# When the keys of short attention blocks are loaded: key loads separated from query loads

## The reference

```python
raw = jnp.einsum('bhid,bhjd->bhij', q, k)
scores = sips_alpha[0] * jnp.tanh(raw / sips_beta[0])
scores = scores + lam * hamming[:, None, :, :]      # soft_bits @ soft_bits.T / 2
scores = scores + lat                               # hexc @ Mh @ hexc.T / 6, per head
scores = jnp.where(causal[None, None], scores, -jnp.inf)
attn = jax.nn.softmax(scores, axis=-1)
out = jnp.einsum('bhij,bhjd->bhid', attn, v)
```

## Time and profile before

| | |
|---|---|
| median of three executions | 1880.96 us |
| profiled execution | 1876.1 us |
| its span, first to last instruction | 1874.3 us |
| TensorE busy | 1736.5 us, 93% |
| VectorE busy | 1309.0 us, 70% |
| ScalarE busy | 1232.2 us, 66% |
| GpSimd busy | 620.1 us, 33% |
| mean granted clock of TensorE | 0.955 |
| moved by DMA | 288.49 MB, 154 GB/s on the mean |

### The profile page before, as it was taken

One profiled execution on the slowest core, in us unless ns is written; L12 is line 12 of the kernel. 1 busy time (PEld: TensorE's weight loads), 2 busy tenths in 40 slices (PEclk: granted clock), 3 DMA queues, 4 the chain that ended last, 5 costly groups with the idle time before them and its releaser, 6 DMA issues. The chain is left out here.

```text
span 1874.3 us, 35368 instructions
## 1 busy us (share of the span) xinstructions
PE 1736.5 (93%) x11140; PEld 1041.4 (56%) x11141; DVE 1309.0 (70%) x2675; ACT 1232.2 (66%) x1260; POOL 620.1 (33%) x715
## 2 busy tenths in 40 slices
PE   4798999999999988999999999899559999999997
PEld 1343434434334433333433334388459999999997
DVE  6467888878888866778877877644646666666664
ACT  1177999999999977789999999633513333333332
POOL 0745251432542453243140201237612222222222
PEclk8778999999999989899999999999879999999998
DMA  4689796676863397676575580172256776767773
GB/s 164 184 218 183 163 173 136 138 148 138 185 112 94 88 182 188 135 158 141 118 158 107 116 179 33 56 233 84 92 189 198 198 197 196 198 198 200 198 202 76
DMA packets 183562, 288.49 MB, mean 154 GB/s; under 512 B 20832, under 2 KB 114144, under 8 KB 181280
## 3 DMA queue, kind: packets, MB, share of 16 engines
q1 hardware_dynamic: 168096, 264.92, 56.4%
q0 software_dynamic: 13440, 17.97, 5.6%
q10 hardware_dynamic: 1920, 4.23, 0.6%
HBM read 218.09 MB, written 68.96 MB: 153 GB/s over the span
## 5 line engine op out<-in xcount | busy, mean ns | idle before, releaser
L1298 DVE SCALAR_TENSOR_TENSOR probs<-probs,scal,bil_ps 128x512 f32<-128x512 f32 (+1 forms) x1152 | 789.4, 715 | 239.2 <-PE bil_ps L1140 187.8
L1219 ACT ACTIVATE probs<-probs 128x2048 f32<-128x2048 f32 (+1 forms) x288 | 522.7, 1815 | 82.6 <-DVE probs L1298 82.0
L1212 ACT ACTIVATE probs<-raw_ps 128x2048 f32<-128x2048 f32 (+1 forms) x288 | 509.1, 1768 | 38.4 <-PE raw_ps L1122 28.6
L1140 PE MATMUL bil_ps<-u_mv,w_st 50*128 50x512 f32 (+3 forms) x1280 | 467.6, 454 | 33.9 <-DVE probs L1298 23.4
L1140 PEld LDWEIGHTS bil_ps<-u_mv,w_st 50*128 50x128 f32 x1280 | 200.1, 188 | 515.1 <-DVE probs L1298 428.3
L2020 ACT ACTIVATE rows_sb<-fc_ps,b 128x128 f32<-128x128 f32 x576 | 160.8, 368 | 345.6 <-DVE hid_lo L2052 304.7
L1159 PE MATMUL o_ps<-probs,v_sb 128*32 128x512 f32 (+3 forms) x2560 | 301.0, 552 | 0.1
L1122 PE MATMUL raw_ps<-q_mv,k_st 64*128 64x512 f32 (+3 forms) x1280 | 271.9, 396 | 13.3 <-ACT probs L1212 9.0
L1976 PE MATMUL fc_ps<-modrow,rows_sb 128*128 128x128 f32 x2304 | 271.6, 277 | 0.0
L1976 PEld LDWEIGHTS fc_ps<-modrow,rows_sb 128*128 128x128 f32 x2304 | 265.5, 194 | 0.0
L1949 POOL DMA_INDIRECT out<-modrow,token x72 | 125.4, 1742 | 379.8 <-DVE modrow L2085 374.0
(11 more groups left out here) (233 smaller groups left out, 1564.4 us busy)
## 6 DMA issues: line engine op xcount, KB each, us to landing
rows_sb<-in_w SPq DMA_DIRECT2D x72, 1024.0 KB, 4.9
q_mv<-q_split SPq DMA_DIRECT2D x128, 128.0 KB, 8.6
k_st<-k_split SPq DMA_DIRECT2D x48, 256.0 KB, 8.7
rows<-x_rows SPq DMA_DIRECT2D x72, 130.0 KB, 2.1
v_rows<-rows_sb SPq DMA_DIRECT2D x8, 1024.0 KB, 7.3
o_t<-o_sb SPq DMA_DIRECT2D x32, 256.0 KB, 7.9
k_st<-k_split SPq DMA_DIRECT2D x16, 512.0 KB, 8.7
v_sb<-v_rows SPq DMA_DIRECT2D x8, 1024.0 KB, 14.7
```

What stands on the lines that cost most here:

```text
L1140: mm = pe.matmul(bil_ps[:, hd % 2, column:column + width], codes(kt)[row:row + BIAS_ROWS, :], u_mv[row:row + BIAS_ROWS, p, hd // 2, query: ...
L1212: act.activation(probs[:, s % NBUF, :, first:BLK], raw_ps[:, :, first:BLK], ACT.Tanh).then_inc(tanh_ready, 1)
L1219: act.activation(scores, scores, ACT.Exp).then_inc(exp_ready, 1)
L1298: dve.scalar_tensor_tensor(scores, scores, scal[:, ALPHA:ALPHA + 1], bil_ps[:, hd % 2, first:BLK], ALU.mult, ALU.add).then_inc(sum_ready, 1)
```

## The change

Keys get loads of their own. Three things change with it.

First, where they lie: in a block with c = 0 the iterations of head groups 0 and 1 use columns 0 to 511 of their side, those of groups 2 and 3 use columns 512 to 1023. With c = 1, groups 0 and 1 use the upper half (columns 1024 to 2047), groups 2 and 3 the lower. Longer blocks use the side as before. KEYS_FREE gives for each iteration the last one before it that used any of its columns; the load waits for that one's raw scores, where it waited for iteration it - 2.

Second, when: the keys of iterations 2 to 5 stand at the same steps (0, 2, 5, 8), with no wait for TensorE. Those of 18 and 19 move from steps 143 and 146 to 128 and 143, those of 20 and 21 from 149 and 152 to 137 and 146. For all others step and wait are the same. The queries stay at the steps and behind the waits where keys and queries were.

Third, semaphores: keys_in has six, by iteration number modulo 6, and the queries have two of their own, so TensorE waits for two at an iteration's start. The keys wait for the stores of keys only, the queries for the stores of queries.

```diff
-KEYS_AT = {max(LAST[it - 2] - PE_LEAD, 0): it for it in range(2, len(ITERS))}
+QUERIES_AT = {max(LAST[it - 2] - PE_LEAD, 0): it for it in range(2, len(ITERS))}
+N_SETS = 6
+def keys_column(it):
+    i, g = ITERS[it]
+    return {0: g // 2 * BLK, 1: (1 - g // 2) * 2 * BLK}.get(BLOCKS[i][1], 0)
+def keys_used(it):
+    first = keys_column(it) // BLK
+    return set((it % 2, n) for n in range(first, first + BLOCKS[ITERS[it][0]][1] + 1))
+KEYS_FREE = {it: max([before for before in range(it) if keys_used(before) & keys_used(it)], default=-1)
+             for it in range(len(ITERS))}
+    step = LAST[it - 2] - PE_LEAD
+    if i == NBLK + 1 and g < 2:
+        stored = max(s for s in STORE_AT if (i, "Q3") in STORE_AT[s])
+        step = max(LAST[KEYS_FREE[it]] + 3, stored + 3)
+    elif i == NBLK and g >= 2:
+        step = LAST[KEYS_FREE[it]] - PE_LEAD + 3
+    KEYS_AT.setdefault(max(step, 0), []).append(it)
...
             def load_keys(it):
-                if it >= 2:
-                    sp.wait_ge(raw_mm, LAST[it - 2] + 1)
-                for m in range(4):
+                if KEYS_FREE[it] >= 0:
+                    sp.wait_ge(raw_mm, LAST[KEYS_FREE[it]] + 1)
+                for m in (2, 3):
                     sp.wait_ge(st_qk[m], 16 * N_QK * (i + 1))
...
+            def load_queries(it):
                 if it >= 2:
                     sp.wait_ge(raw_mm, LAST[it - 2] + 1)
+                for m in (0, 1):
                     sp.wait_ge(st_qk[m], 16 * N_QK * (i + 1))
...
-                if s in KEYS_AT:
-                    load_keys(KEYS_AT[s])
+                for it in KEYS_AT.get(s, []):
+                    load_keys(it)
+                if s in QUERIES_AT:
+                    load_queries(QUERIES_AT[s])
...
-                    pe.wait_ge(keys_in[p], 16 * N_KEYS * (it // 2 + 1))
+                    pe.wait_ge(keys_in[it % N_SETS], 16 * N_KEYS * (it // N_SETS + 1))
+                    pe.wait_ge(queries_in[p], 16 * N_QUERIES * (it // 2 + 1))
...
-                                       k_st[row:row + ROWS, p, hd // 2, kt * P:(kt + 1) * P],
+                                       k_st[row:row + ROWS, p, hd // 2, keys_column(it) + kt * P:keys_column(it) + (kt + 1) * P],
```

More of the change, by code:

```diff
@@ L228 @@
 GATES_AT = 9
-KEYS_AT = {max(LAST[it - 2] - PE_LEAD, 0): it for it in range(2, len(ITERS))}
+QUERIES_AT = {max(LAST[it - 2] - PE_LEAD, 0): it for it in range(2, len(ITERS))}
[8 more added lines that the diff above has]
+             for it in range(len(ITERS))}
+KEYS_AT = {}
+for it in range(2, len(ITERS)):
+    i, g = ITERS[it]
+    step = LAST[it - 2] - PE_LEAD
[5 more added lines that the diff above has]
+    KEYS_AT.setdefault(max(step, 0), []).append(it)
 BIAS_AT = {LAST[it - 2] - PE_LEAD + 1: it for it in range(2, len(ITERS))}
@@ L587, in stage_front @@
         st_w, st_s, st_l, st_g, st_v = sem("st_w"), sem("st_s"), sem("st_l"), sem("st_g"), sem("st_v")
-        keys_in = [sem(f"keys_in{p}") for p in range(2)]
+        keys_in = [sem(f"keys_in{p}") for p in range(N_SETS)]
+        queries_in = [sem(f"queries_in{p}") for p in range(2)]
         bias_in = [sem(f"bias_in{p}") for p in range(2)]
@@ L605, in stage_front @@
         N_QK, N_W, N_S, N_L, N_G, N_V = 2, 4, 4, 4, 2, 1
[L606 removed]
+        N_KEYS, N_QUERIES, N_BIAS, N_CODES = 6, 4, 6, 2
         N_EARLY = 5
@@ L706, in load_keys @@
                 i, g = ITERS[it]
+                c, p, first = BLOCKS[i][1], it % 2, keys_column(it)
+                if KEYS_FREE[it] >= 0:
+                    sp.wait_ge(raw_mm, LAST[KEYS_FREE[it]] + 1)
+                for m in (2, 3):
+                    sp.wait_ge(st_qk[m], 16 * N_QK * (i + 1))
+                seen, place = slice(0, (c + 1) * BLK), slice(first, first + (c + 1) * BLK)
+                k_both = heads("k_split", 2 * HD, i, g, seen).rearrange("(j z r) t -> z r j t", z=2, r=2 * HD)
+                k_rows = heads("k_split", 2 * HD, i, g, seen).rearrange("(j z s r) t -> z s r j t", z=2, s=2, r=HD)
+                load = lambda dst, src: sp.dma_start(dst.bitcast(F32), src).then_inc(keys_in[it % N_SETS], 16)
+                for z in range(2):
+                    row = z * ROWS
+                    load(k_st[row:row + 2 * HD, p, :, place], k_both[z])
+                    load(k_st[row + 2 * HD:row + 3 * HD, p, :, place], k_rows[z, 1])
+                    load(k_st[row + 3 * HD:row + 4 * HD, p, :, place], k_rows[z, 0])
+            def load_queries(it):
+                i, g = ITERS[it]
                 c, p = BLOCKS[i][1], it % 2
@@ L709, in load_keys @@
                     sp.wait_ge(raw_mm, LAST[it - 2] + 1)
-                for m in range(4):
+                for m in (0, 1):
                     sp.wait_ge(st_qk[m], 16 * N_QK * (i + 1))
-                seen, own = slice(0, (c + 1) * BLK), slice(c * BLK, (c + 1) * BLK)
-                k_both = heads("k_split", 2 * HD, i, g, seen).rearrange("(j z r) t -> z r j t", z=2, r=2 * HD)
-                k_rows = heads("k_split", 2 * HD, i, g, seen).rearrange("(j z s r) t -> z s r j t", z=2, s=2, r=HD)
+                own = slice(c * BLK, (c + 1) * BLK)
                 q_rows = heads("q_split", 2 * HD, i, g, own).rearrange("(j z r) t -> z r j t", z=2, r=2 * HD)
-                load = lambda dst, src: sp.dma_start(dst.bitcast(F32), src).then_inc(keys_in[p], 16)
                 for z in range(2):
[L718 to L721, removed]
                     for half in range(2):
-                        load(q_mv[row + half * 2 * HD:row + (half + 1) * 2 * HD, p, :, :], q_rows[z])
+                        row = z * ROWS + half * 2 * HD
+                        sp.dma_start(q_mv[row:row + 2 * HD, p, :, :].bitcast(F32), q_rows[z]
+                                     ).then_inc(queries_in[p], 16)
             def load_bias(it):
@@ L839, in _ @@
             load_keys(0)
+            load_queries(0)
             store(0, "V1")
@@ L847, in _ @@
             load_keys(1)
+            load_queries(1)
             load_bias(1)
```

## The result

The changed kernel took 1870.41 us (median of five, 1865.32 to 1872.38), the kernel before 1880.96 (1873.17 to 1882.50): ratio 0.9942, interval 0.9918 to 0.9966. It is 0.6% faster, 10.6 us. The profiled execution, 1872.38, is the slowest of the five; its span is 1870.6.

The account below looks back on a forecast made before the run. TensorE, 93% busy, was paced mostly by ScalarE and VectorE, with two load stalls costing 20.0 us in all. 1876.1 - 7 (A) - 10 (B) = 1859, so 1861 for a typical run; range 1852 to 1875.

Parts of the forecast that it names:

- the first rival: Iterations 20 and 21: only A goes, the denominators stay late by nearly as much; gain 9, 1869 us; chance 0.20.
- A: Iteration 20's first step: TensorE's 4.68 us wait for bias rows goes once iteration 20's keys move; gain 7 us.
- B: Iteration 21: VectorE's 8.00 us wait for block 4's denominators (den) shrinks or goes; gain 10 us, within 5 to 12.5.
- its own signs: Iterations 18 to 21: den's wait below 2 us, iteration 21 26 to 30; wrong if their sum falls under 11.
- the drained end: Iteration 21: queue drained when iteration 22's keys go out, den lands at 725 after 6.0 us, nothing waits.
- the queue-limited end: Iteration 21: full engines keep 32.8 us from x_o's issue to den's landing, at 735.2, 4.2 us late.
- The second: Iterations 20 and 21: the stall only moves, A halves and B stays; gain 3, 1875 us; chance 0.14.
- The third: Iteration 19: early keys 21 delay its bias rows, TensorE stands 8 us, 3 us slow clock; 1889 us; chance 0.06.
- The parts costed at nothing: All iterations: split store waits and one more TensorE wait at 31 iteration starts; nothing, or 1.6 us hidden.
- The first blocks: Iterations 2 to 5: keys no longer wait for TensorE, keys 2 up to 7 us sooner; gain 0 to 2, taken 0.

Follow-up runs that it names:

- only_20: Against the kernel before: split loads and semaphores kept, but only the keys of iteration 20 moved earlier, into the upper half; 1871.95 us, ratio 0.9960.
- old_21: Changed kernel with only the keys of iteration 21 back at step 152, behind bias 20 and the old wait; 1871.24 us, ratio 0.9946.
- before_den: Kernel before with only the load of block 4's denominators two steps sooner, ahead of iteration 22's keys; 1870.12 us, ratio 0.9940.
- den_ahead: Changed kernel with the load of block 4's denominators two steps sooner, ahead of iteration 22's keys; 1862.52 us, ratio 0.9929.
- split_only: Against the kernel before: only the split loads, waits and semaphores, with keys at their old columns and steps; 1874.79 us, ratio 0.9980.
- rep_after: The changed kernel run again with no edit; 1866.24 us, ratio 0.9948 against the kernel before.

## Why the prediction came out as it did

**In short.** The number lies inside its range, but in part by luck: 20 us below the median of before were forecast and 10.6 came, and the range held this because it took in the first rival (1869). Of the two terms A came true and B did not. By its own signs the forecast failed: den's wait is 3.6 and 3.7 us (below 2), iteration 21 lasts 33.15 and 31.60 us (26 to 30), and iterations 18 to 21 together fell from 91.2 us, the mean of three profiles, to 81.9, the mean of two, 9.2 us where it asked for 11. The other signs came true: a DMA share of 0.46 before the middle, no wait for `u_mv` at iteration 20, and none for a DMA at iteration 19.

**Stall A was right.** Expected were no wait and iteration 20 at 26 to 28 us; every kernel with keys 20 early has 26.05 to 26.09. Against the mean of the three profiles of before (33.39) this is a gain of 7.3, forecast 7. only_20 shows that keys 20 do it alone.

**The step that failed is the size of stall B,** taken as 10 with bounds 5 and 12.5. Its working was right up to the choice. x_o was to go out 13.8 us after iteration 20's first tanh (702.4 against 688.6); it did at 13.76. From there two ends were given, the same 32.8 us to den's landing, 4.2 us late, or a drained queue and no wait. I chose near the drained end, with den issued 7.5 us after keys 22 and landed 6.0 us later, because the 6.0 us of the earlier trace rows seemed to come from the crowd itself. In after it was issued 727.53 - 713.75 = 13.8 us after them and took 13.8. The load of 6.0 us, at 671.80, had none of the transfers of eight late parts close ahead of it: of these stores and loads the kernel before issues none between 640 and 704. The measured x_o to den was 32.3 and 32.8 us and the wait 3.6 and 3.7: the queue-limited end, within 0.6 us. Nine executions with den behind keys 22 gave 31.5 to 32.8 us, whatever lay before x_o. The wait is then (x_o's place + 31.5 to 32.8) less the 42.5 us after iteration 20's first tanh at which VectorE asks; old_21's 16.75 gives 5.8 to 7.1, measured 7.04. (Where A stays, VectorE asks later, at 48.7 to 50.8.)

**A second error lies in the base.** B's wait in the profiled execution was 8.0 us, in two others 6.1 and 4.0. Iterations 21 and 22 together last 65.62, 60.67 and 58.20 us in before, mean 61.5, and 63.75 and 58.22 in the changed kernel, mean 61.0. On these few profiles B gave 0.5 us, not 10 (against the profiled execution alone, 1.9 and 7.4). A stall read from one execution was taken as the stall of all of them.

**Together.** From iteration 16 to 24 the three profiles of before mean 165.4 us, the two of the changed kernel 157.9: 7.5 us gained, and 1 us or so at the start. The medians differ by 10.6 and 13.3 us, the intervals reach down to about 6. The five profiled executions themselves differ by 9.8 us in the mean of their spans, so 8.5 of these lie between 16 and 24 and at the start; the rest isn't assigned, with spreads of 8.5 and 9.9 us between profiles of one kernel.

**The rivals.** The first, only A goes (1869), is what happened to the time, and its reason holds in good part: den's time hangs on what is issued between x_o and den, as before_den and den_ahead show, and its late half comes in right behind the stores of queries or keys. The Trainium skill (DMA: Bandwidth & Descriptors, Queues, rings and completion order) has the descriptors of a queue taken in ring order on each DMA engine. By that rule each part of den waits for what was issued ahead of it on its engine; these traces agree, with 20 us after x_o against 32. The Trainium skill (DMA: Bandwidth & Descriptors, Rules for kernel authors) has a DMA with an outermost dimension of 8 confined to at most 8 engines. The traces agree: such stores leave eight late parts, and den's second eight come 0.2 to 0.9 us behind them. The prediction had no row of single engines; the record of the semaphores comes near to one. What stays open is how the time would be with stores of another shape. The second, half of A only, is refuted by 26.06. The third, keys 21 delay bias 19, had a small true core: one wait of 2.59 us in five profiles, not the 8 us and the 1889 forecast; only_20 had 2.74 us without keys 21 ahead. (That wait was for bias 18.) The 14.45 us of iteration 19 in after looked like it and were not, for no DMA was waited for.

**The parts costed at nothing** held: the added waits at iteration starts show in no profile, and split_only isn't slower. The first blocks: iteration 4 opens at 151.1 us on the mean of the three profiles of before and at 150.1 in the two of the changed kernel. Between 80 and 160 us TensorE's waits for queries are gone (3.1, 11.3 and 9.4 us in the three of before, none in after, rep_after and split_only), those for bias rows stay (2.8, 9.1 and 11.3 us, then 11.0, 10.3 and 10.6). Of the query waits some 1 us came out at iteration 4's start, within the 0 to 2 of the forecast and too small to tell from nothing.

## What to carry to other kernels

When several loads share one queue, cost a late one by the queue: take the time from the issue of a fixed landmark to its landing, and assume it stays unless what stands between them changes. Then ask by how many DMA engines each neighbour goes: a load that uses all of them has landed only when its slowest part has. The cheapest cure for a small load that something waits for is then its place in the list: two steps for a 32 KB load gave 11 us in the kernel before, as much as the rearranged loads of 3 MB of keys. And read a stall in two or three executions before its whole size enters a sum.

## What the runs showed of the hardware

In all thirteen profiles most iterations repeat within 0.1 us, whatever stood before them. Iterations 8, 24 and 27 vary by 1.2 to 1.6 us; larger differences arise only in iterations 0 to 4 and 18 to 22. The DMA engines are full there (shares of 1.0 to 1.1 in many of the windows), but that alone isn't it: the share was 0.96 in 230 to 280 of before too, and iteration 7, which lies in it, repeats within 0.02 us.

A load that goes by all DMA engines can have half of its parts in after 2.2 us and the last after 15.5 (den in den_ahead), when transfers that go by eight of them stand ahead of it.

A short wait can cost far more than its length, and differently each time, by the clock behind it. The wait of 3.6 us in after and of 3.7 in rep_after made iterations 21 and 22 11.3 and 5.7 us longer than in den_ahead. These are the windows of after behind the wait:

```profile
745.00:755.00 10.00, 10.00 (x34) 3.48 (x37) 4.73 (x8) 5.32 (x4) 3.46 (x6) 0.50 0.43 114
755.00:765.00 10.00, 10.00 (x42) 3.59 (x36) 4.64 (x8) 5.47 (x4) 4.38 (x5) 0.54 0.46 162
```

TensorE is busy all of the time and gets 1.2 GHz for most of it, with no load waited for. It was granted 1.00 in 730 to 740, before the wait. In rep_after the slow stretch behind the wait is shorter (0.75 in 732 to 740, 0.86 in 740 to 750), which is where the two executions differ. In iteration 19 the clock fell in the same way with no wait ahead (0.54 in 680 to 690 of after), in some executions and not in others of one kernel (14.45 and 10.53 us); why stays open.

SP's issue of one and the same kind of DMA can take 0.35 us or 6.3, which delays all behind it. These are two output stores of rep_after, the first where the DMA share is 0.79 (726 to 732), the second where it is 0.20 (757 to 765). That the fuller queue is the reason is argued from this and not shown:

```profile
725.77 6.27 SPq L813 DMA_DIRECT2D o_t<-o_sb  x1
...
757.39 0.35 SPq L813 DMA_DIRECT2D o_t<-o_sb  x1
```
